# Attention on TensorE: key steps taken in pairs, transposes two steps ahead

## The chip, the cores and the metric

The kernel runs on one core of a Trainium2 chip. The metric is the device time of one execution in microseconds (us). A core has TensorE (PE in the profile; PEld is its loading of weights), VectorE (DVE), ScalarE (ACT), GpSimd (POOL) and SyncE (SP), which issues the DMAs. Each engine works through its own instructions in order and waits on semaphores that other engines raise.

## The reference

A decoder layer: a sparse gated block, cross attention over 1601 keys, and an expert block, each followed by a layer norm. The change lies in the attention, whose core is this, with 32 query heads on 8 key heads of 128, four batches of 256 rows, and keys and queries normalized:

```python
k = _rmsnorm(jnp.repeat(k, GROUPS, axis=1), k_norm_w)
scores = jnp.einsum('bhqd,bhkd->bhqk', q, k) * scale
scores = scores + attention_mask[:, :, :, :kv_len]
probs = jax.nn.softmax(scores.astype(jnp.float32), axis=-1).astype(q.dtype)
out = jnp.einsum('bhqk,bhkd->bhqd', probs, v)
```

## The kernel before, in words

Every product in fp32 precision is made of three products of rounded parts: a number is split into a high part (fp32r) and the low part that is left, and `product` issues high by high, high by low and low by high.

Attention runs over 64 **units**. A unit is half of an item (a batch and a key head): 2 heads x 256 rows, that is four **tiles** j = 0 to 3 of 128 rows by 1601 keys. The hardware loop has trips of four units (`BODY`), u = 0 to 3, and a last trip written out. Within a unit every engine goes through the 13 key steps kt = 0 to 12 (`NT`) of 128 keys, the last of 65, and calls its own `position(i, u, kt)` for each. What an engine does at a position, and in which order, is written by hand:

- PE: `score` at the positions of `AT` (kt 0: tile 1 of the next unit; kt 2: tile 2; kt 5: tile 3; kt 10: tile 0 of the unit after the next): four banks of 402 keys, 12 products, into PSUM banks 0 to 3, which wait for the mask subtraction of the tile before. `weigh_values(kt)`: three products of 512 columns that add values times probabilities to bank 7. `transpose_p`: four transposes of 128 x 128 that turn a step's probabilities of the four tiles into one of three banks (`t_bank`, 4 to 6, in turn). They run `LAG` = 3 steps ahead of the value step, and step 0 of a unit waits (`p_done`) until all four tiles of that unit are normalized. Before it writes a bank, a transpose waits until the low part of the step that used it last is done; in a trip of 52 steps the turn of three doesn't close, so step 0 of a trip waits for the step just before.
- DVE: at kt 0, 3, 5, 8 (`INVERT_AT`) a reciprocal of a tile's sum; at `AT` the mask subtraction with running minimum (`subtract_mask`, L1526), which frees the score's banks; then `split_p`: the low part pT_lo (L1565) of the step that was transposed at this position. For four of the 13 steps (`BY_VECTOR`, the step behind each of `AT`'s positions) DVE also makes the high copy pT_hi (L1561).
- ACT: the high copy pT_hi of the other nine steps (L1495); at kt 12 the copy of bank 7 to o_sb (L1509); at `AT` the exponential of the tile whose mask was subtracted (L1473); at kt 1, 4 and 9 the high part of keys, queries or values of a coming item (`splits`, L1461, L1467).
- POOL: at `INVERT_AT` the product of a tile with its reciprocal (`normalize`, L1419), then low parts of keys, queries or values.
- SP: loads and stores, at kt 1 and kt 12.

The values of a step need its low part (`pT_lo_done`); the splits write into a ring of four (`RING`).

Of the kernel before, what the change touches and what calls it, by code (L numbers as in the profile page):

```python
# [67 lines left out]
def done(step):  # L68

    return AHEAD + 1 + step  # L70
# [42 lines left out]
class Chip:  # L113
# [9 lines left out]
    def sem(self, name):  # L123

        if name not in self.sems:
            self.sems[name] = self.ctx.enter_context(self.nc.semaphore(name))
        return self.sems[name]
# [26 lines left out]
def product(pe, out, a_hi, a_lo, b_hi, b_lo, start, stop):  # L154


    pe.matmul(out, a_hi, b_hi, start=start, stop=False)  # L157
    pe.matmul(out, a_hi, b_lo, start=False, stop=False)  # L158
    return pe.matmul(out, a_lo, b_hi, start=False, stop=stop)  # L159
# [837 lines left out]


def queries(chip, x1T_hi, x1T_lo, WqT, qn, kn, qS, attention):


# [4 lines left out]
    TRIPS = G // 2  # L1006
    LAG = 3
    w_raw = chip.raw[:, 0:2 * CT * W].rearrange("p (r c n) -> p r c n", r=2, c=CT)
# [28 lines left out]
    def last_trip(i):  # L1037
        return isinstance(i, int) and i == TRIPS - 1
# [4 lines left out]
    def upcoming(i, s):  # L1043


        if not last_trip(i) or s + LAG < TT:
            return s + LAG
        return s + LAG - 1 if TT <= s + LAG - 1 < BODY else None

# [57 lines left out]
    def squares(act, i, s):  # L1107
        n = BODY * i + s
        act.wait_ge(q_done, done(n))
        act.wait_ge(ssq_done, done(n - 2))  # L1110
        for h in range(HG):
            last = act.activation(square[:, s % 2, h * HD:(h + 1) * HD], psum[:, bank(i, s), h * HD:(h + 1) * HD],
                                  ACT.Square, accum_out=ssq[:, s % TT, h:h + 1])
        last.then_inc(ssq_done, 1)
# [5 lines left out]
    def scalar(act):  # L1120
# [9 lines left out]

        for s in range(1, LAG):
            squares(act, 0, s)
# [88 lines left out]
def attention(chip, mask, qS, kS, vS, oS, output):  # L1221
# [5 lines left out]
    sem, psum, ident, raw = chip.sem, chip.psum, chip.ident, chip.raw  # L1227
# [4 lines left out]
    SB, SW = 4, 402  # L1232
    KP = SB * SW
    NT = (KV + P - 1) // P
    KR = KV - (NT - 1) * P
    LAG = 3
    TB = 3
    RING = 4
    BODY = 4
    TRIPS = UNITS // BODY  # L1240
    AT = {0: 1, 2: 2, 5: 3, 10: 0}
    INVERT_AT = {0: 0, 3: 1, 5: 2, 8: 3}


    BY_VECTOR = sorted((at + 1 + LAG) % NT for at in AT)
    BY_SCALAR = [kt for kt in range(NT) if kt not in BY_VECTOR]
# [22 lines left out]

    def t_bank(m):  # L1270

        return psum[:, SB + m % (NT * BODY) % TB, :]

    mask_in, k_in, q_in, v_in = (sem(name) for name in ("mask_in", "k_in", "q_in", "v_in"))
    pads, mask_done = sem("pads_a"), sem("mask_done")
# [4 lines left out]
    pT_done, pT_lo_done = sem("pT_done"), sem("pT_lo_done")  # L1280
# [11 lines left out]
    def rows(kt):  # L1292
        return P if kt < NT - 1 else KR

    def schedule(eng, position):

        with eng.Fori(0, TRIPS - 1) as i:
            for u in range(BODY):
                for kt in range(NT):
                    position(i, u, kt)  # L1300
        for u in range(BODY):
            for kt in range(NT):
                position(TRIPS - 1, u, kt)

    def last_trip(i):
        return isinstance(i, int) and i == TRIPS - 1

    def exists(i, u):
        return u < BODY or not last_trip(i)

    def scored(u, kt):

        return (u + 1, AT[kt]) if AT[kt] else (u + 2, 0)

    def transposed(u, kt):

        return (u, kt + LAG) if kt + LAG < NT else (u + 1, kt + LAG - NT)

    def tile(i, u, j):
        return QT * (BODY * i + u) + j  # L1320

    def key_step(i, u, kt):
        return NT * (BODY * i + u) + kt

    def share_step(i, u, kt, share):

        return len(share) * (BODY * i + u) + share.index(kt)
# [194 lines left out]
    def subtract_mask(dve, i, u, j, spare=0):  # L1522
        n = QT * (u % 2) + j

        wait_apart(dve, s_done, done(tile(i, u, j)), dve_passed)
        dve.tensor_tensor_reduce(banked(p_sb[u % 2][:, j]), psum[:, 0:SB, 0:SW],  # L1526
                                 banked(minus_mask[:, j % 2]), 1.0, 3.4028235e38, ALU.add, ALU.min, t_min[:, n:n + 1]
                                 ).then_inc(t_done, 1)

    def invert(dve, i, u, j):  # L1530
        n = QT * (u % 2) + j
        dve.wait_ge(e_done, done(tile(i, u, j)))
        dve.reciprocal(p_inv[:, n:n + 1], p_sum[:, n:n + 1]).then_inc(inv_done, 1)  # L1533
# [21 lines left out]
    def vector(dve):  # L1555
        def split_p(i, u, kt):
            m, n = NT * u + kt, key_step(i, u, kt)
            if kt in BY_VECTOR:
                dve.wait_ge(pT_done, done(n))
                dve.wait_ge(pv_done, done(n - RING))  # L1560
                dve.tensor_copy(pT_hi[0:rows(kt), m % RING], t_bank(m)[0:rows(kt)]).then_inc(pT_hi_dve, 1)  # L1561
                dve.wait_ge(pT_hi_dve, done(share_step(i, u, kt, BY_VECTOR)))
            else:
                dve.wait_ge(pT_hi_act, done(share_step(i, u, kt, BY_SCALAR)))
            dve.tensor_tensor(pT_lo[0:rows(kt), m % RING], t_bank(m)[0:rows(kt)],  # L1565
                              pT_hi[0:rows(kt), m % RING].bitcast(F32), ALU.subtract).then_inc(pT_lo_done, 1)

        def position(i, u, kt):
            if kt in INVERT_AT and exists(i, u + 1):
                invert(dve, i, u + 1, INVERT_AT[kt])  # L1570
            if kt in AT and exists(i, scored(u, kt)[0]):
                subtract_mask(dve, i, *scored(u, kt))
            if exists(i, transposed(u, kt)[0]):
                split_p(i, *transposed(u, kt))
            if last_trip(i) and u >= BODY - 2:
                output.early["vector"](dve, u - BODY, kt)

        for kt in range(LAG):
            split_p(0, 0, kt)
        schedule(dve, position)  # L1580

    def score(pe, i, u, j):
        slot, q = u // 2 % 2, slice(QW * (u % 2) + P * j, QW * (u % 2) + P * (j + 1))
        if j == 0 and u % 2 == 0:
            pe.wait_ge(kq_lo, done(len(KQ) * (2 * i + u // 2 + 1) - 1))
        pe.wait_ge(t_done, done(tile(i, u, j) - 1))
        for b in range(SB):
            k = slice(SW * b, SW * (b + 1))
            last = product(pe, psum[:, b, 0:SW], q_hi[slot][:, q], q_lo[slot][:, q],
                           k_hi[slot][:, k], k_lo[slot][:, k], True, True)  # L1590
        last.then_inc(s_done, 1)
# [9 lines left out]
    def tensor(pe):  # L1601
        def transpose_p(i, u, kt):
            m, n = NT * u + kt, key_step(i, u, kt)
            if kt == 0:
                pe.wait_ge(p_done, done(tile(i, u, QT - 1)))

            pe.wait_ge(pT_lo_done, done(n - 1 if m % (NT * BODY) == 0 else n - TB))
            for j in range(QT):
                last = pe.transpose(t_bank(m)[0:rows(kt), P * j:P * (j + 1)],  # L1609
                                    p_sb[u % 2][:, j, P * kt:P * kt + rows(kt)], ident)  # L1610
            last.then_inc(pT_done, 1)

        def weigh_values(i, u, kt):
            m, n, slot = NT * u + kt, key_step(i, u, kt), u // 2 % 2
            r, d = rows(kt), slice(HD * kt, HD * (kt + 1))
            if kt == 0:
                pe.wait_ge(v_lo_done, done(len(V) * (2 * i + u // 2 + 1) - 1))
                pe.wait_ge(o_done, done(BODY * i + u - 1))
            pe.wait_ge(pT_lo_done, done(n))
            product(pe, o_ps, v_hi[slot][0:r, d], v_lo[slot][0:r, d], pT_hi[0:r, m % RING], pT_lo[0:r, m % RING],  # L1620
                    kt == 0, kt == NT - 1).then_inc(pv_done, 1)

        def position(i, u, kt):
            if kt in AT and exists(i, scored(u, kt)[0]):
                score(pe, i, *scored(u, kt))
            weigh_values(i, u, kt)
            if exists(i, transposed(u, kt)[0]):
                transpose_p(i, *transposed(u, kt))

        pe.wait_ge(sem("qT_sb_done"), done(TT * G - 1))  # L1630
        for kt in range(LAG):
            transpose_p(0, 0, kt)
        schedule(pe, position)

    def open_counts(eng, which):
# [302 lines left out]
def decoder_layer(nc, x, xT, ctxT, mask, WgT, WuT, WdT, WqT, WkT, WvT, WoT, qn, kn, routeT, AT, BwT, out):  # L1938
# [7 lines left out]
    with ExitStack() as whole:  # L1946
# [5 lines left out]

        output = output_and_experts(chip, oS, x1S, WoT, AT, routeT, BwT, out)
        attend = attention(chip, mask, qS.rearrange("b g d h q -> (b g) d (h q)"), kS, vS, oS, output)
        query = queries(chip, x1T_hi, x1T_lo, WqT, qn, kn, qS, attend)
        down = down_and_norm(chip, abs_s, x1T_hi, x1T_lo, x, WdT, pS, x1S, k_sb, query)
# [98 lines left out]
```

## Time and profile before

| | us |
|---|---|
| median of 3 runs | 2784.19 (2783.2 to 2784.31) |
| the profiled execution | 2784.38 |
| its span in the trace | 2782.6 |
| first and last transpose of attention (L1609) | 1059.4 and 2564.6 |
| mean granted clock of TensorE | 0.995 |

The page of a profile gives each engine's busy time as a share of the span; the stretches further down split it by time. A busy PE means that a matmul was in flight. The timeline gives each instruction's start and length. Matmuls overlap, so that the cost of one is the distance from its start to the start of the next.

### The profile page before, as it was taken

What the parts mean: (1) busy time and instruction counts of PE and PEld (TensorE: products, weight loads), DVE (VectorE), ACT (ScalarE), POOL (GpSimd) and SP (SyncE); (2) the same over time, 40 slices, a digit from 0 to 9 for tenths busy, and PEclk for the clock granted to TensorE, in tenths of its full rate; (3) what the DMA queues carried; (4) which work ended last, traced back from release to release, by engine and by line L of the source; (5) the groups of instructions that cost most, each with busy time, mean ns of one, the idle gap of its engine ahead of it and who ended that gap; (6) DMA issues with size and microseconds to landing.
All of it is one profiled execution on the core that took longest, in us unless ns stands there. A gap on an engine that the chain in (4) does not pass through costs nothing.

```text
span 2782.6 us, 45351 instructions
## 1 busy us (share of the span) xinstructions
PE 2738.6 (98%) x14624; PEld 2366.3 (85%) x14624; DVE 2055.9 (74%) x3054; ACT 1362.6 (49%) x2992; POOL 1024.7 (37%) x756
## 2 busy tenths in 40 slices
PE   8999999999999999999999999999999999999998
PEld 7888888888788878889988998988998889888786
DVE  2289999988855566777777777777777777777543
ACT  3243333333424445665666656665666566654421
POOL 1122222222403345454454544454545454541000
PEclk9999999999999999999999999999999999999999
DMA  5253333333333442111111111111111111111632
GB/s 176 81 175 111 104 113 113 106 109 106 97 125 116 125 131 82 63 54 62 54 62 54 62 54 62 54 62 54 61 54 48 57 52 60 54 43 64 205 107 72
DMA packets 252783, 239.49 MB, mean 86 GB/s; under 512 B 12084, under 2 KB 210772, under 8 KB 252728
## 3 DMA queue, kind: packets, MB, share of 16 engines
q1 hardware_dynamic: 252728, 238.81, 27.3%
q8 instruction: 28, 0.46, 0.1%
q14 instruction: 27, 0.22, 0.0%
HBM read 142.92 MB, written 95.85 MB: 86 GB/s over the span
## 4 chain that ended last, share of the span: by engine, by line
PE 96%; issue 2%; POOL 1%; DVE 1%; ACT 0%; DMA 0%; POOLq 0%; SPq 0%; DVEq 0%; ACTq 0%
PE banks L157 27%; PE banks L159 26%; PE banks L158 26%; PE banks L1609 13%; PE banks L323 2%; PE banks L1195 1%; PE banks L930 0%; POOL rstd_q L1095 0%; PE banks L1919 0%; PE banks L1929 0%; DVE p_even L1526 0%; DMA raw<-WoT_in 0%; POOL p_even L1419 0%; POOL x_lo L228 0%; DVE wo_lo L1818 0%
## 5 line engine op out<-in xcount | busy, mean ns | idle before, releaser
L1565 DVE TENSOR_TENSOR pT_lo<-banks,pT_hi 128x512 fp32r<-128x512 f32 (+1 forms) x832 | 573.3, 689 | 111.6 <-ACT pT_hi L1495 94.4
L1495 ACT CAST pT_hi<-banks 128x512 fp32r<-128x512 f32 (+1 forms) x576 | 334.3, 581 | 531.6 <-PE banks L1609 531.5
L560 DVE TENSOR_SCALAR_CACHE_REDUCE flags<-abs_s,cand 128x1376 bf16<-128x1376 f32 x248 | 393.3, 1642 | 1.1
L157 PE MATMUL banks<-pT_hi,v_hi 128*128 128x512 f32 (+1 forms) x832 | 376.1, 452 | 2.9 <-DVE pT_lo L1565 1.6
L157 PE MATMUL banks<-k_hi,q_hi 128*128 128x402 f32 x1024 | 378.8, 370 | 0.0
L158 PE MATMUL banks<-k_lo,q_hi 128*128 128x402 f32 x1024 | 355.4, 347 | 0.0
L159 PE MATMUL banks<-k_hi,q_lo 128*128 128x402 f32 x1024 | 354.3, 346 | 0.0
L159 PE MATMUL banks<-pT_hi,v_lo 128*128 128x512 f32 (+1 forms) x832 | 327.9, 394 | 0.0
L158 PE MATMUL banks<-pT_lo,v_hi 128*128 128x512 f32 (+1 forms) x832 | 326.9, 393 | 0.0
L157 PE MATMUL banks<-kvw_hi,c_hi 128*128 128x512 f32 x816 | 326.1, 400 | 0.0
L158 PE MATMUL banks<-kvw_lo,c_hi 128*128 128x512 f32 x816 | 321.9, 394 | 0.0
L159 PE MATMUL banks<-kvw_hi,c_lo 128*128 128x512 f32 x816 | 321.9, 394 | 0.0
L1419 POOL TENSOR_SCALAR p_even<-p_even,p_inv 128x1601 f32<-128x1601 f32 x128 | 207.2, 1618 | 310.9 <-DVE p_inv L1533 310.9
L1526 DVE CUSTOM_DVE_ANT_0 p_odd<-banks,minus_mask 128x1608 f32<-128x1608 f32 x128 | 234.5, 1832 | 105.5 <-PE banks L159 105.5
L1526 DVE CUSTOM_DVE_ANT_0 p_even<-banks,minus_mask 128x1608 f32<-128x1608 f32 x128 | 234.5, 1832 | 103.5 <-PE banks L159 103.5
L1419 POOL TENSOR_SCALAR p_odd<-p_odd,p_inv 128x1601 f32<-128x1601 f32 x128 | 207.5, 1621 | 211.2 <-DVE p_inv L1533 211.1
L1609 PEld LDWEIGHTS banks<-ident,p_even 128*128 128x128 f32 (+1 forms) x1664 | 207.7, 140 | 58.2 <-DVE qT_sb L1161 2.0
L1609 PEld LDWEIGHTS banks<-ident,p_odd 128*128 128x128 f32 (+1 forms) x1664 | 206.9, 140 | 56.9 <-POOL p_odd L1419 1.0
L1609 PE MATMUL banks<-ident,p_even 128*128 128x128 f32 (+1 forms) x1664 | 249.9, 273 | 1.8 <-DVE qT_sb L1161 1.8
L1609 PE MATMUL banks<-ident,p_odd 128*128 128x128 f32 (+1 forms) x1664 | 249.3, 272 | 0.6 <-POOL p_odd L1419 0.6
L1473 ACT ACTIVATE p_odd<-p_odd,t_min 128x1601 f32<-128x1601 f32 x128 | 209.6, 1637 | 39.9 <-DVE t_min L1526 39.9
L1473 ACT ACTIVATE p_even<-p_even,t_min 128x1601 f32<-128x1601 f32 x128 | 209.6, 1638 | 29.3 <-DVE t_min L1526 29.3
(162 smaller groups left out, 5330.5 us busy)
## 6 DMA issues: line engine op xcount, KB each, us to landing
raw<-keys SPq DMA_DIRECT2D x32, 800.5 KB, 4.5
values<-v_sb SPq DMA_DIRECT2D x50, 512.0 KB, 2.6
keys<-kT_sb SPq DMA_DIRECT2D x50, 512.0 KB, 4.5
raw<-values SPq DMA_DIRECT2D x32, 768.0 KB
queries<-qT_sb SPq DMA_DIRECT2D x64, 256.0 KB, 2.6
raw<-queries SPq DMA_DIRECT2D x32, 512.0 KB, 5.1
attended<-o_sb SPq DMA_DIRECT2D x128, 128.0 KB, 1.8
raw<-attended SPq DMA_DIRECT2D x64, 256.0 KB, 2.9
```

Source lines behind the costliest of these rows:

```text
L157: pe.matmul(out, a_hi, b_hi, start=start, stop=False)
L158: pe.matmul(out, a_hi, b_lo, start=False, stop=False)
L159: return pe.matmul(out, a_lo, b_hi, start=False, stop=stop)
L323: last = pe.transpose(banks[:, g * P:(g + 1) * P], k_sb[:, g * HD:(g + 1) * HD], chip.ident)
L560: bits.done(dve.tensor_scalar(flags[:, tt % 2], abs_s[:, tt], at[:, tt:tt + 1].bitcast(F32), 0.0, ALU.is_lt, ALU.add, accum_out=out[:, tt: ...
L1195: last = pe.transpose(psum[:, bank(i, s), h * P:(h + 1) * P], q_sb[:, s % 4, h * HD:(h + 1) * HD], ident)
L1419: pool.tensor_scalar(at, at, p_inv[:, n:n + 1], 1.0, ALU.mult, ALU.mult).then_inc(p_done, 1)
L1473: act.activation(at, at, ACT.Exp, bias=t_min[:, n:n + 1], scale=-1.0, accum_out=p_sum[:, n:n + 1]).then_inc(e_done, 1)
L1495: act.copy(pT_hi[0:rows(kt), m % RING], t_bank(m)[0:rows(kt)]).then_inc(pT_hi_act, 1)
L1526: dve.tensor_tensor_reduce(banked(p_sb[u % 2][:, j]), psum[:, 0:SB, 0:SW], banked(minus_mask[:, j % 2]), 1.0, 3.4028235e38, ALU.add, ALU.m ...
L1565: dve.tensor_tensor(pT_lo[0:rows(kt), m % RING], t_bank(m)[0:rows(kt)], pT_hi[0:rows(kt), m % RING].bitcast(F32), ALU.subtract).then_inc(p ...
L1609: last = pe.transpose(t_bank(m)[0:rows(kt), P * j:P * (j + 1)], p_sb[u % 2][:, j, P * kt:P * kt + rows(kt)], ident)
```

## The change

The transposes run two steps ahead (`LAG` = 2). PE takes the steps in pairs: at every even step m = 13u + kt it does two transpose groups one after the other, steps m + 2 and m + 3, eight transposes, then the value steps m and m + 1, six products. In units with even u these are the even kt, in the others the odd ones. A score stands ahead of the transposes of its position, except tile 0 (kt 10), which stands behind them. With `LAG` the four steps that DVE copies move from 1, 4, 6, 9 to 0, 3, 5, 8. At odd m, and at kt 10, DVE does the split ahead of the mask subtraction. The last step of a trip uses bank 1 of the three in place of bank 0, and waits for the step two before it.

```diff
--- before.py
+++ after.py
@@ -1233,7 +1233,7 @@
     KP = SB * SW
     NT = (KV + P - 1) // P
     KR = KV - (NT - 1) * P
-    LAG = 3
+    LAG = 2
     TB = 3
     RING = 4
     BODY = 4
@@ -1269,7 +1269,12 @@
 
     def t_bank(m):
 
-        return psum[:, SB + m % (NT * BODY) % TB, :]
+        turn = m % (NT * BODY)
+        return psum[:, SB + (1 if turn == NT * BODY - 1 else turn % TB), :]
+
+    def t_bank_last(m):
+
+        return {NT * BODY - 1: 2, 0: 4, 1: 2, 2: 4}.get(m % (NT * BODY), TB)
 
     mask_in, k_in, q_in, v_in = (sem(name) for name in ("mask_in", "k_in", "q_in", "v_in"))
     pads, mask_done = sem("pads_a"), sem("mask_done")
@@ -1568,9 +1573,12 @@
         def position(i, u, kt):
             if kt in INVERT_AT and exists(i, u + 1):
                 invert(dve, i, u + 1, INVERT_AT[kt])
+            turned_first = (NT * u + kt) % 2 or AT.get(kt) == 0
+            if turned_first and exists(i, transposed(u, kt)[0]):
+                split_p(i, *transposed(u, kt))
             if kt in AT and exists(i, scored(u, kt)[0]):
                 subtract_mask(dve, i, *scored(u, kt))
-            if exists(i, transposed(u, kt)[0]):
+            if not turned_first and exists(i, transposed(u, kt)[0]):
                 split_p(i, *transposed(u, kt))
             if last_trip(i) and u >= BODY - 2:
                 output.early["vector"](dve, u - BODY, kt)
@@ -1604,7 +1612,7 @@
             if kt == 0:
                 pe.wait_ge(p_done, done(tile(i, u, QT - 1)))
 
-            pe.wait_ge(pT_lo_done, done(n - 1 if m % (NT * BODY) == 0 else n - TB))
+            pe.wait_ge(pT_lo_done, done(n - t_bank_last(m)))
             for j in range(QT):
                 last = pe.transpose(t_bank(m)[0:rows(kt), P * j:P * (j + 1)],
                                     p_sb[u % 2][:, j, P * kt:P * kt + rows(kt)], ident)
@@ -1621,11 +1629,21 @@
                     kt == 0, kt == NT - 1).then_inc(pv_done, 1)
 
         def position(i, u, kt):
-            if kt in AT and exists(i, scored(u, kt)[0]):
-                score(pe, i, *scored(u, kt))
+
+            m = NT * u + kt
+            def scores():
+                if kt in AT and exists(i, scored(u, kt)[0]):
+                    score(pe, i, *scored(u, kt))
+
+            if AT.get(kt) != 0:
+                scores()
+            if m % 2 == 0:
+                for ahead in (transposed(u, kt), transposed((m + 1) // NT, (m + 1) % NT)):
+                    if exists(i, ahead[0]):
+                        transpose_p(i, *ahead)
+            if AT.get(kt) == 0:
+                scores()
             weigh_values(i, u, kt)
-            if exists(i, transposed(u, kt)[0]):
-                transpose_p(i, *transposed(u, kt))
 
         pe.wait_ge(sem("qT_sb_done"), done(TT * G - 1))
         for kt in range(LAG):
```

## Rows read from the trace of the kernel before

**Rows 1.** The page, part 1: TensorE's busy time, share of the span, instructions.
```profile
PE 2738.6 (98%) x14624; PEld 2366.3 (85%) x14624; DVE 2055.9 (74%) x3054; ACT 1362.6 (49%) x2992; POOL 1024.7 (37%) x756
```

**Rows 2.** Busy us (x instructions) by engine in the middle of attention, clock, DMA.
```profile
1500.00:2000.00 500.00, 500.00 (x2943) 449.62 (x2942) 394.47 (x614) 302.43 (x434) 244.59 (x139) 1.00 0.18 56
```

**Rows 3.** Timeline, start us and length us: PE's blocks in attention.
```profile
1600.01 0.60 PE L1609 MATMUL banks<-ident,p_even 128*128 128x128 f32 x4
...
1600.36 0.48 PE L157 MATMUL banks<-pT_hi,v_hi 128*128 128x512 f32 x1
...
1600.67 0.39 PE L158 MATMUL banks<-pT_lo,v_hi 128*128 128x512 f32 x1
...
1600.91 0.40 PE L159 MATMUL banks<-pT_hi,v_lo 128*128 128x512 f32 x1
...
1601.14 0.60 PE L1609 MATMUL banks<-ident,p_even 128*65 128x128 f32 x4
...
1601.50 0.43 PE L157 MATMUL banks<-k_hi,q_hi 128*128 128x402 f32 x1
...
1603.78 0.39 PE L157 MATMUL banks<-pT_hi,v_hi 128*128 128x512 f32 x1
```

**Rows 4.** Timeline of PE in the stage of keys: eight transposes in a row.
```profile
500.84 1.03 PE L323 MATMUL banks<-ident,k_sb 128*128 128x128 f32 x8
...
501.63 0.48 PE L157 MATMUL banks<-kvw_hi,c_hi 128*128 128x512 f32 x1
...
501.95 0.39 PE L158 MATMUL banks<-kvw_lo,c_hi 128*128 128x512 f32 x1
```

**Rows 5.** Timeline of an even unit: from score j=3 to the next unit.
```profile
1595.90 0.39 PE L157 MATMUL banks<-pT_hi,v_hi 128*128 128x512 f32 x1
...
1596.26 1.83 DVE L1526 CUSTOM_DVE_ANT_0 p_odd<-banks,minus_mask 128x1608 f32<-128x1608 f32 x1 [0.74 <-PE banks L159]
...
1598.02 0.69 DVE L1565 TENSOR_TENSOR pT_lo<-banks,pT_hi 128x512 fp32r<-128x512 f32 x1
...
1598.13 1.64 ACT L1473 ACTIVATE p_odd<-p_odd,t_min 128x1601 f32<-128x1601 f32 x1 [0.24 <-DVE t_min L1526]
...
1598.62 0.68 DVE L1561 CAST pT_hi<-banks 128x512 fp32r<-128x512 f32 x1
...
1599.33 0.69 DVE L1565 TENSOR_TENSOR pT_lo<-banks,pT_hi 128x512 fp32r<-128x512 f32 x1
...
1599.76 0.57 ACT L1495 CAST pT_hi<-banks 128x512 fp32r<-128x512 f32 x1
...
1600.36 0.69 DVE L1565 TENSOR_TENSOR pT_lo<-banks,pT_hi 128x512 fp32r<-128x512 f32 x1 [0.34 <-ACT pT_hi L1495]
...
1600.97 0.15 DVE L1533 RECIPROCAL p_inv<-p_sum 128x1 f32<-128x1 f32 x1
...
1601.33 1.62 POOL L1419 TENSOR_SCALAR p_odd<-p_odd,p_inv 128x1601 f32<-128x1601 f32 x1 [2.17 <-DVE p_inv L1533]
...
1604.48 0.60 PE L1609 MATMUL banks<-ident,p_odd 128*128 128x128 f32 x4
```

**Rows 6.** Timeline of the odd unit behind it: ACT and DVE round score j=1.
```profile
1607.63 0.57 ACT L1495 CAST pT_hi<-banks 128x512 fp32r<-128x512 f32 x1
...
1608.10 0.59 ACT L1509 COPY o_sb<-banks 128x512 f32<-128x512 f32 x1
...
1608.23 0.69 DVE L1565 TENSOR_TENSOR pT_lo<-banks,pT_hi 128x512 fp32r<-128x512 f32 x1 [0.34 <-ACT pT_hi L1495]
...
1609.74 1.83 DVE L1526 CUSTOM_DVE_ANT_0 p_even<-banks,minus_mask 128x1608 f32<-128x1608 f32 x1 [0.74 <-PE banks L159]
...
1611.61 1.64 ACT L1473 ACTIVATE p_even<-p_even,t_min 128x1601 f32<-128x1601 f32 x1 [0.24 <-DVE t_min L1526]
...
1611.63 0.45 PE L157 MATMUL banks<-k_hi,q_hi 128*128 128x402 f32 x1
...
1613.24 0.85 ACT L1461 CAST k_hi<-raw 128x804 fp32r<-128x804 f32 x1
```

## The prediction

> **What bounds the kernel now.** I read the page first. TensorE is busy for 98% of the span [rows 1]. Then the busy time by stretch: in the middle of attention PE shows 500.00 us of 500, at granted clock 1.00, while DVE shows 394, ACT 302 and POOL 245 [rows 2]. So PE's own work sets attention's time, and a change helps only if it makes that work shorter. It hurts as soon as PE waits, even for an engine that is idle a fifth of the time. That stretch has 2943 products and transposes; a unit (one pass over 13 key steps, with four score tiles) has 48 + 39 + 52 = 139, so a unit takes 500 / (2943/139) = 23.6 us, and the 64 units 1,511 us.
>
> The timeline of PE gives the price of each block from start to start, better than the recorded durations, which overlap. Between the starts of two transpose groups lie 1.13 us (1600.01 to 1601.14) [rows 3]. The three value products start at 1600.36, .67 and .91 and the next group 0.23 later: 0.31, 0.24, 0.23. The first looks 0.08 slow, but its record begins only 0.35 us after the group's start, where four transposes at a pitch of 0.11 would end after 0.44. So the 0.08 belongs to the transposes: a group is 0.436 us, the three products 0.697, together 1.13. A score is twelve products, from 1601.50 to 1603.78, less the same 0.08: 2.20. A unit by these is 4 x 2.20 + 13 x 1.133 = 23.53, so there is less than 0.1 us of waiting in 23.6.
>
> **The change, part by part.** Nothing is computed that wasn't, no DMA moves, and SP's and POOL's queues keep their order. Three things change.
>
> *Pairs of transpose groups.* They halve the passages between transposes and products. What is a passage worth? Another stage of this kernel has eight transposes in a row [rows 4]: 0.79 us to the record of the product behind them, 0.32 to the next. That is 1.11, less a product's 0.23: 0.88 for eight, or 0.110 each. Four in a row cost 0.35 + 0.31 - 0.23 = 0.43, 0.108 each. A passage costs nothing either way, so halving them gains 0. The other bound is to believe the 0.08 us: 416 passages fewer x 0.08 = 33 us gained. I take 0; the row of eight shows the very same 0.08. The Trainium skill (TensorE: Matmul & The Clock Gate, LDWEIGHTS) puts a load of 128 columns at 128/1.2 = 107 ns, whatever else; the pitch of 0.11 agrees, and by it transposes are bound by their loads and the sum's term is also 0.
>
> *LAG 2, the order of the pairs and the four steps that VectorE copies (0, 3, 5, 8 in place of 1, 4, 6, 9).* This changes what lies between a score and the work that hangs on it. The prices of the links are those of the trace, from start to start [rows 5, 6]: score's end to DVE's mask subtraction 0.36 (1595.90 to 1596.26); that to ACT's exponential 1.87, to the next work on DVE about 1.76, to the score that waited for it 1.89 (1609.74 to 1611.63); exponential to the next ACT copy 1.63; copy to the next copy 0.47; copy to DVE's low part 0.60; a DVE copy to its own low part 0.71; a low part to the next DVE instruction 0.61, to PE 0.69 + 0.06 = 0.75 (the 0.06 is what the score needed after the 1.83 of the subtraction); reciprocal to POOL 0.36; POOL's product 1.62.
>
> I call a unit even or odd by u. In an even unit the pairs stand at kt 0, 2, 4 ... 12, in an odd one at 1, 3 ... 11. Going round the two, each wait on PE in turn:
>
> (a) Even unit, kt 5 to 10. From the end of score j=3 the chain is 0.36 + 1.87 + 1.63 + 0.60 (ACT copies step 9 only after the exponential) + 0.61 (DVE reciprocal) + 0.36 + 1.62 + 0.05 = 7.10. In the rows it is 1595.90 to 1601.33 + 1.62 = 1602.95, the same 7.05 [rows 5]. Who waits: the first transposes of the next unit, which need all four normalized tiles. Now they start at 1604.48, 1.5 us after POOL's end, because score j=0 and value step 10 come before them. In the changed kernel they come before both. PE has between: values 5 to 9 and transposes 8 to 12, that is 5 x 0.697 + 5 x 0.436 = 5.67. PE is late by 7.10 - 5.67 = 1.43. In it lie two earlier waits, for the low parts of steps 8 and 9 (3.57 against 3.40 for the second group of the pair at kt 8; 5.21 for value step 9 against 4.70). Behind the waiting transpose stand the score j=0 and everything else on PE, so nothing fills the hole. 1.43 per pair of units.
>
> (b) From that score j=0's end to score j=3 in the odd unit. DVE subtracts at 0.36, the exponential starts at 2.23. Behind it on ACT are, in order, the copy of step 1 (3.86), the copy of o_sb (4.33), the copy of step 2 (4.80). In an odd unit DVE takes step 2 ahead of the subtraction j=1 (the new `turned_first`): low part at 5.40, subtraction at 6.01, where the score's end plus 0.36 would be 5.52. It goes on: exponential 7.88 (score j=2 starts at 7.9), on ACT k_hi (9.51, length 0.85), then the copy of step 4 at 10.3; its low part 10.9 stands again ahead of subtraction j=2: 11.5 instead of 10.5. Score j=3 may start at 11.5 + 1.89 = 13.4. PE's work to there is 8 values, 6 transpose groups, 2 scores: 5.58 + 2.62 + 4.40 = 12.60. Late by 0.8, of which score j=2 waits 0.5 already. Before, the same place cost 0.08. So +0.75.
>
> (c) Odd unit, kt 7. After score j=3 the subtraction starts at 0.7 (DVE still has step 6) and is ahead of step 7's low part, 2.45 to 3.20. The pair at kt 7 needs it for its second group, which PE reaches at 2.7: 0.5. Value step 8 then waits 0.15 more for DVE's copy and low part of step 8. With LAG 3 both had a step more of room. +0.65.
>
> (d) Even unit, kt 4: the second group needs step 4's low part, whose subtraction j=2 came first on DVE: score's end + 0.36 + 1.75 + 0.75 = 2.86, against 2 values, 3 groups = 2.70. +0.16.
>
> *The banks.* The last step of a trip now takes bank 1 and waits for the step two before it in place of three. That step's transposes come in the pair right behind score j=3's chain (c); its low part is about 0.6 us later than PE asks. 16 trips: 16 x 0.6 = 9 us. Nothing covers it, since value step 9, score j=0 and the next unit stand behind it.
>
> Where it costs nothing: value steps 0 to 3, 10, 11 and 12 find their low parts done, since a score (2.20 us) stands between; the first transposes of an even unit come behind a score and value 10, so (a) doesn't appear there; o_sb is copied while score j=1 runs. Their cover is that 2.20 us; without it each would cost up to 0.5 us.
>
> **The sum.** Per two units 1.43 + 0.75 + 0.65 + 0.16 = 2.99 us; 32 of these are 96 us; the banks add 9. The profiled execution took 2784.38 us (span 2782.6) and the median is 2784.19, so nothing is corrected between them: 2784 + 105 = 2889. Bounds: (a) alone is the term whose whole chain stands in the rows, 32 x 1.43 = 46 us, 2830. If each wait also pays for a restart of PE, at most the 0.08 that score j=2 loses now, some 7 waits x 0.08 x 32 = 18 us more: 2908.
>
> **The rivals.**
> R1, only (a) bites. The waits of (b), (c) and (d) come from order on DVE and ACT, and PE is by then later than planned, which gives these engines room that I count only once. For it: DVE is 79% busy, it catches up. Against it: their chains begin at scores, so they shift with PE. 2830 to 2850. Chance 0.18.
> R2, the other side: a passage between transposes and products does cost the 0.08 us and the chains are shorter than I make them. 2784 - 33 = 2751. It decides only if a pair's second group of transposes is followed without loss and (a) is under 1.0 us. Against it: the row of eight [rows 4], and 7.05 us read off directly. 0.05.
> R3, the order does nothing that counts: PE's sequence stays full and passages are free, 2784. It needs slack of 1.4 us at (a) which the rows don't have. 0.05.
> R4, PE's clock falls. The Trainium skill (TensorE: Matmul & The Clock Gate, Part 4) says that transposes don't count as activity for the clock gate. By rows: the clock is 1.00 over 500 us with 37% of the instructions transposes [rows 2], and the change adds none. My waits are below 1.5 us each. Were the clock at half in a tenth of attention, that stretch would cost its own length again, up to 150 us: above 2920. 0.04.
> My forecast, the sum within 2850 to 2920: 0.68.
>
> **The numbers.** 2889 is the likeliest. R1 and the forecast together hold 0.86; from 2828 to 2915 leaves out R2, R3, R4 and the outermost of the forecast, under 2 in 10. Measurement can tell about 0.2%, 5.6 us. Faster 0.05 (R2), same 0.05 (R3), slower 0.90.
>
> **What would show it.** Transpose groups of eight at a pitch of 0.11 and the products behind them with the same 0.48 us record; PE idle at the first transposes of every second unit, released by POOL's normalization, 0.8 us or so there and 1.4 in all since score j=3; waits of scores j=2 and j=3 in odd units for DVE; a period of two units near 50.2 us in place of 47.2; the stages before and after unchanged. I am wrong if PE stays at 100% of attention, if the pitch in groups of eight is below 0.10, or if DVE gets through its queue sooner than the links say.

## The result, and the profile after

The changed kernel takes 2891.22 us (median of 4 runs, 2890.77 to 2892.85), the kernel before 2783.69 on the same chip (4 runs, 2782.29 to 2784.31): a ratio of 1.0388, 95% interval 1.037 to 1.0406. The profiled execution took 2890.95 us.

The page: span, and part 1 (busy time by engine).

```profile
span 2889.2 us, 45396 instructions
...
PE 2795.0 (97%) x14624; PEld 2365.4 (82%) x14624; DVE 2051.9 (71%) x3054; ACT 1339.1 (46%) x2992; POOL 1023.8 (35%) x756
```

The same stretch as in [rows 2], of the changed kernel.

```profile
1500.00:2000.00 500.00, 484.51 (x2741) 418.78 (x2740) 366.36 (x573) 276.31 (x405) 229.50 (x129) 1.00 0.17 53
```

Where 2943 matmuls fitted into 500 us there are 2741, at the same clock: a unit takes 500 / (2741/139) = 25.36 us in place of 23.6, so 1.74 x 64 = 111 us if the whole stage went like this stretch (the stage is measured below). PE isn't full any more (484.51 of 500), and DVE is *less* busy than before. The instructions of the other engines didn't get slower: the mask subtraction takes 1.82 to 1.83 us, the exponential 1.64 and POOL's product 1.61, as before. PE waits.

**Eight transposes in a row** (timeline of PE, changed kernel):

```profile
1600.18 1.03 PE L1617 MATMUL banks<-ident,p_odd 128*128 128x128 f32 x8
1600.97 0.48 PE L157 MATMUL banks<-pT_hi,v_hi 128*128 128x512 f32 x1
1601.29 0.39 PE L158 MATMUL banks<-pT_lo,v_hi 128*128 128x512 f32 x1
```

Start to start 0.79 and 0.32: what the eight of the stage of keys took [rows 4], and per transpose what four took [rows 3]. A pair saves nothing.

**The even unit behind score j=3** (timeline; start, length, and in brackets the idle time and its releaser), against [rows 5]:

```profile
1588.33 1.53 ACT L1500 CAST pT_hi<-banks 128x512 fp32r<-128x512 f32 x3
...
1588.92 0.69 DVE L1570 TENSOR_TENSOR pT_lo<-banks,pT_hi 128x512 fp32r<-128x512 f32 x1 [0.93 <-ACT pT_hi L1500]
...
1589.53 0.15 DVE L1538 RECIPROCAL p_inv<-p_sum 128x1 f32<-128x1 f32 x1
...
1589.67 0.50 PE L157 MATMUL banks<-pT_hi,v_hi 128*128 128x512 f32 x1 [0.27 <-DVE pT_lo L1570]
...
1589.89 1.61 POOL L1424 TENSOR_SCALAR p_odd<-p_odd,p_inv 128x1601 f32<-128x1601 f32 x1 [2.78 <-DVE p_inv L1538]
...
1591.63 0.65 PE L1617 MATMUL banks<-ident,p_odd 128*128 128x128 f32 x4 [0.57 <-POOL p_odd L1424]
```

Three ACT copies sit merged in the first line, since they had waited behind the exponential. Value step 9 starts when step 9's low part (1588.92) is done. The reciprocal, 0.36 behind it POOL, and 1.74 behind POOL's start the transposes of the next unit: 1589.53, 1589.89, 1591.63. Before, those transposes started 1.5 us after POOL's end [rows 5]; now they start 0.13 us after it.

**The odd unit behind it** (timeline of ACT, DVE and PE), against [rows 6]:

```profile
1598.19 0.56 ACT L1500 CAST pT_hi<-banks 128x512 fp32r<-128x512 f32 x1
...
1598.66 0.58 ACT L1514 COPY o_sb<-banks 128x512 f32<-128x512 f32 x1
...
1599.13 0.59 ACT L1500 CAST pT_hi<-banks 128x512 fp32r<-128x512 f32 x1
...
1599.76 0.69 DVE L1570 TENSOR_TENSOR pT_lo<-banks,pT_hi 128x512 fp32r<-128x512 f32 x1 [0.21 <-ACT pT_hi L1500]
...
1600.37 1.82 DVE L1531 CUSTOM_DVE_ANT_0 p_even<-banks,minus_mask 128x1608 f32<-128x1608 f32 x1
...
1602.23 1.64 ACT L1478 ACTIVATE p_even<-p_even,t_min 128x1601 f32<-128x1601 f32 x1 [2.51 <-DVE t_min L1531]
...
1602.26 0.46 PE L157 MATMUL banks<-k_hi,q_hi 128*128 128x402 f32 x1 [0.34 <-DVE t_min L1531]
...
1603.87 0.85 ACT L1466 CAST k_hi<-raw 128x804 fp32r<-128x804 f32 x1
...
1605.23 0.69 DVE L1570 TENSOR_TENSOR pT_lo<-banks,pT_hi 128x512 fp32r<-128x512 f32 x1 [1.70 <-ACT pT_hi L1500]
...
1605.84 1.82 DVE L1531 CUSTOM_DVE_ANT_0 p_even<-banks,minus_mask 128x1608 f32<-128x1608 f32 x1
...
1607.72 0.45 PE L157 MATMUL banks<-k_hi,q_hi 128*128 128x402 f32 x1
```

Behind the exponential come the copy of step 1, the copy of o_sb, the copy of step 2, its low part at 1599.76, and only then the subtraction at 1600.37. The score j=1 ended where value step 0 starts, at 1599.49, and 0.36 behind that would have been 1599.85. Score j=2 starts at 1602.26, 1.89 after the subtraction. Once more: k_hi (1603.87) holds up step 4's copy on ACT, its low part (1605.23) stands ahead of the subtraction (1605.84), and score j=3 waits until 1607.72.

**The other places** (timeline of PE: kt 7 and 8 of that odd unit, where the second transpose group starts 0.79 behind the first in place of 0.44; then kt 9 of the last unit of a trip, where it is 0.91, the wait for a bank):

```profile
1612.30 0.60 PE L1617 MATMUL banks<-ident,p_odd 128*128 128x128 f32 x4
1613.09 0.66 PE L1617 MATMUL banks<-ident,p_odd 128*128 128x128 f32 x4 [0.19 <-DVE pT_lo L1570]
1613.50 0.47 PE L157 MATMUL banks<-pT_hi,v_hi 128*128 128x512 f32 x1
...
1614.41 0.50 PE L157 MATMUL banks<-pT_hi,v_hi 128*128 128x512 f32 x1
```

```profile
1665.65 0.60 PE L1617 MATMUL banks<-ident,p_odd 128*128 128x128 f32 x4
1666.56 0.65 PE L1617 MATMUL banks<-ident,p_odd 128*65 128x128 f32 x4 [0.30 <-DVE pT_lo L1570]
```

Who waited for whom in attention (us in total, times, longest):

```profile
PE banks L1617 <- POOL p_odd L1424: 17.6, 32, 0.6
PE banks L1617 <- DVE pT_lo L1570: 15.1, 48, 2.7
PE banks L157 <- DVE t_min L1531: 10.4, 31, 0.3
PE banks L157 <- DVE pT_lo L1570: 9.1, 33, 0.4
```

These rows add up to 52 us, half of what was lost. The record of a value product lasts 0.39 us where the next starts 0.23 behind it, so the recorded ends reach some 0.16 us beyond the slot, and a wait is partly or wholly covered by its forerunner's record. The loss has to be read from starts. I did that for all 1,915 blocks of PE in attention, with the prices of the prediction (group 0.436, three products 0.697, score 2.20; behind transposes the start is taken from the second product): each block's start less the former's start and price. A block right behind a waiting one starts 0.06 us late by this measure as well; that is the 0.06 in the rows.

| place | predicted, us | measured mean, us |
|---|---|---|
| (a) even: second group at kt 8, value 8, value 9, first transposes of the next unit | 1.43 | 0.18 + 0.06 + 0.54 + 0.71 = 1.49 |
| (b) odd: scores j=2, j=3, less 0.09 before | 0.75 | 0.61 + 0.29 - 0.09 = 0.81 |
| (c) odd: second group at kt 7, values 7 and 8 | 0.65 | 0.34 + 0.06 + 0.23 = 0.63 |
| (d) even: second group at kt 4, value 4 | 0.16 | 0.16 + 0.06 = 0.22 |
| banks, once a trip | 0.6 | 0.46 |
| all of attention | 105 | 122.7 - 13.9 = 108.8 |

The 13.9 are the same sum in the kernel before; 5.5 of it is score j=2's wait, most of the rest lies in the first and the last unit. From the start of attention's first block to that of its last it is 1508.0 us before and 1616.9 after, the same difference. The places (a) to (d) and the banks make 32 x 3.15 + 16 x 0.46 = 108 us of it. The rest of the span is 2.3 us shorter than before, so that the profiled executions differ by 106.6. The banks' 0.46 is the typical value, found in 15 of the 16 trips; in the last one, which is written out, it is 1.98 us, and the shortened exponential further down leaves it there.

### The profile page after: what moved, and what is told of

Read it like the earlier page. It is cut to its first block, busy times and chain, and to the rows that moved or that the text cites. A ratio compares the mean times of both kernels' runs of the same rounds, so it can differ in the third digit from the quotient of the medians.

```text
span 2889.2 us, 45396 instructions
## 1 busy us (share of the span) xinstructions
PE 2795.0 (97%) x14624; PEld 2365.4 (82%) x14624; DVE 2051.9 (71%) x3054; ACT 1339.1 (46%) x2992; POOL 1023.8 (35%) x756
## 4 chain that ended last, share of the span: by engine, by line
PE 82%; issue 8%; ACT 3%; DVE 3%; POOL 3%; DMA 0%; ACTq 0%; DVEq 0%; POOLq 0%; SPq 0%
PE banks L157 23%; PE banks L159 23%; PE banks L158 23%; PE banks L1617 10%; ACT pT_hi L1500 2%; POOL p_odd L1424 2%; PE banks L323 2%; DVE p_even L1531 1%; DVE pT_lo L1570 1%; PE banks L1195 1%; ACT o_sb L1514 1%; DVE p_inv L1538 0%; PE banks L930 0%; ACT p_even L1478 0%; POOL rstd_q L1095 0%
## 5 line engine op out<-in xcount | busy, mean ns | idle before, releaser
L1500 ACT CAST pT_hi<-banks 128x512 fp32r<-128x512 f32 (+1 forms) x576 | 323.7, 580 | 123.7 <-PE banks L1617 121.1
L157 PE MATMUL banks<-k_hi,q_hi 128*128 128x402 f32 x1024 | 368.0, 359 | 11.4 <-DVE t_min L1531 10.4
L157 PE MATMUL banks<-pT_hi,v_hi 128*128 128x512 f32 (+1 forms) x832 | 367.1, 441 | 9.8 <-DVE pT_lo L1570 9.1
L1617 PE MATMUL banks<-ident,p_odd 128*128 128x128 f32 (+1 forms) x1664 | 229.9, 275 | 29.6 <-POOL p_odd L1424 17.6
L1617 PEld LDWEIGHTS banks<-ident,p_odd 128*128 128x128 f32 (+1 forms) x1664 | 191.6, 140 | 71.5 <-DVE pT_lo L1570 46.9
L1617 PE MATMUL banks<-ident,p_even 128*128 128x128 f32 (+1 forms) x1664 | 232.3, 275 | 5.5 <-DVE pT_lo L1570 3.1
L157 PEld LDWEIGHTS banks<-k_hi,q_hi 128*128 128x128 f32 x1024 | 193.2, 189 | 51.5 <-DVE t_min L1531 46.0
```

Source lines behind the costliest of these rows:

```text
L1500: act.copy(pT_hi[0:rows(kt), m % RING], t_bank(m)[0:rows(kt)]).then_inc(pT_hi_act, 1)
```

## The experiments

Theory A is the prediction's: PE's blocks need low parts, free banks and normalized tiles whose chains begin at a score; the new order asks for them sooner, and PE waits for the difference. Theory B is that one of the two halves of the change alone is the cause, first the pairs, then the shorter lead. Ratios are to the kernel before, run on the same chip.

**Lead alone.** LAG 2 in the kernel before, no pairs; tile 0's score and subtraction behind the transposes of kt 10.

```diff
-    LAG = 3
+    LAG = 2
...
-            if kt in AT and exists(i, scored(u, kt)[0]):
+            if AT.get(kt) and exists(i, scored(u, kt)[0]):
                 score(pe, i, *scored(u, kt))
             weigh_values(i, u, kt)
             if exists(i, transposed(u, kt)[0]):
                 transpose_p(i, *transposed(u, kt))
+            if AT.get(kt) == 0 and exists(i, scored(u, kt)[0]):
+                score(pe, i, *scored(u, kt))
...
+            turned_first = AT.get(kt) == 0
+            if turned_first and exists(i, transposed(u, kt)[0]):
+                split_p(i, *transposed(u, kt))
             if kt in AT and exists(i, scored(u, kt)[0]):
                 subtract_mask(dve, i, *scored(u, kt))
-            if exists(i, transposed(u, kt)[0]):
+            if not turned_first and exists(i, transposed(u, kt)[0]):
```

> The kernel before with LAG 2 and no pairs; only tile 0's score and its mask subtraction go behind the transposes of kt 10, which need their data. Theory A (the loss comes from work that hangs on a score and now has a step less of room): behind score j=3 value step 7 waits 0.6 us and step 8 0.2, behind j=2 step 4 waits 0.6, score j=2 itself 0.3; 1.6 us a unit more than before, 64 units, so about 2885 us, as much as the changed kernel, though there are no pairs. PE waits for low parts, none for POOL's normalization. Theory B (it is the pairs themselves: eight transposes and then six products hold PE's partners up): 2784 to 2800 us.

Measured: 2956.82 us, ratio 1.0621 (1.0605 to 1.0637). That the pairs alone are the cause falls: without a pair the loss is not smaller but 66 us larger. Yet my size missed by 72 us. The waits of this kernel in attention, and one of them in PE's timeline:

```profile
PE banks L157 <- DVE pT_lo L1565: 67.4, 180, 1.6
...
PE banks L157 <- ACT o_sb L1509: 20.5, 60, 1.2
```

```profile
1607.85 0.60 PE L1612 MATMUL banks<-ident,p_even 128*128 128x128 f32 x4
1608.88 0.50 PE L157 MATMUL banks<-pT_hi,v_hi 128*128 128x512 f32 x1 [0.43 <-DVE pT_lo L1565]
```

By block starts each unit loses 2.8 us, where I had 1.7 with what it lost before: value steps 4 and 7 wait 0.69 each (I said 0.6), step 8 0.19; score j=2, from which I expected 0.3, doesn't wait; but step 9 waits 0.41 and step 10 0.12, which I had missed, and value step 0 waits 0.60 for ACT's copy of o_sb, which stands behind the exponential. In the changed kernel value step 10 stands behind tile 0's score, here ahead of it, so that 0.7 us less work lies between that score and value step 0; and a pair's two groups lie between a score and the values that follow in half of the cases. So the short lead costs by itself. That the changed kernel loses less with the same lead fits these differences of order, but no run separates them.

**Pairs with the old lead.** The changed kernel with LAG 3, tile 0's score ahead of the transposes again, and with it its mask subtraction in even units. With LAG the four steps that DVE copies move back to 1, 4, 6, 9.

```diff
-    LAG = 2
+    LAG = 3
...
-            turned_first = (NT * u + kt) % 2 or AT.get(kt) == 0
+            turned_first = (NT * u + kt) % 2
...
-            if AT.get(kt) != 0:
-                scores()
+            scores()
             if m % 2 == 0:
...
-            if AT.get(kt) == 0:
-                scores()
```

> The changed kernel with LAG 3: pairs of steps m + 3 and m + 4. Theory A: the lead of three doesn't save it, since the second of a pair comes up to a step earlier than before. The first transposes of a unit now stand in odd units at kt 9, 4.97 us behind score j=3, with the chain to POOL's end at 7.1: a wait of 2.1 us there; scores j=2 and j=3 of odd units 1.1 in all, 0.6 more in small waits: some 3.8 us per two units, about 2900 us (2870 to 2920). Theory B (the loss is the shorter lead alone, pairs are harmless): 2784 to 2800 us. A theory that passages cost 0.08 us each would give 2751 where no wait is added.

Measured: 2888.89 us, ratio 1.038 (1.0365 to 1.0396), 11 us less than I expected. Its largest wait in attention:

```profile
PE banks L1617 <- POOL p_even L1424: 48.8, 31, 1.8
```

The first transposes, now at kt 9 of odd units, lose 1.76 us by block starts (I said 2.1), score j=3 of odd units 0.30 and score j=2 nothing new (I said 1.1 for both), small waits and the banks the rest. Lead 3 doesn't save pairs: the first transposes of a unit are pulled ahead of tile 0's score in one unit of two, by either way. So that the shorter lead alone is the cause falls too. Each half of the change by itself costs as much as the whole or more (lead 174 us, pairs 106, both 107): they don't add. That fits Theory A, as both take away blocks of PE between a score and the work that hangs on it.

**The chain to POOL, made shorter.** Changed kernel, tile 3's reciprocal and normalization at kt 7.

```diff
-    INVERT_AT = {0: 0, 3: 1, 5: 2, 8: 3}
+    INVERT_AT = {0: 0, 3: 1, 5: 2, 7: 3}
```

> The changed kernel, with the reciprocal and normalization of tile 3 at kt 7 in place of kt 8, ahead of step 9's split on DVE. Theory A: the chain behind score j=3 gets about 1 us shorter (7.1 to 6.1), the wait for POOL at the first transposes of an odd unit goes, the one of value step 9 (0.5) stays: 0.75 us less in each of 32 even units, 24 us, so about 2867 us. If POOL's end isn't what PE waits for there, 2891 us.

Measured: 2865.56 us, ratio 1.03 (1.0286 to 1.0314): 25.7 us less than the changed kernel. Timeline round the first transposes, and what PE still waits for in attention:

```profile
1580.73 0.17 DVE L1538 RECIPROCAL p_inv<-p_sum 128x1 f32<-128x1 f32 x1 [0.47 <-ACT p_odd L1478]
...
1581.10 1.62 POOL L1424 TENSOR_SCALAR p_odd<-p_odd,p_inv 128x1601 f32<-128x1601 f32 x1 [1.73 <-DVE p_inv L1538]
...
1583.18 0.60 PE L1617 MATMUL banks<-ident,p_odd 128*128 128x128 f32 x4
```

```profile
PE banks L1617 <- DVE pT_lo L1570: 13.6, 49, 1.8
...
PE banks L157 <- DVE t_min L1531: 10.2, 31, 0.4
PE banks L157 <- DVE pT_lo L1570: 9.2, 33, 0.4
```

POOL starts at 1581.10 and ends at 1582.72; the transposes follow at 1583.18 without a wait, and the row for POOL is gone. By block starts 0.71 falls to nothing, value step 9 keeps its 0.54.

**The same wait, covered instead.** Changed kernel, tile 0's score between the two groups of kt 10 in even units.

```diff
-                for ahead in (transposed(u, kt), transposed((m + 1) // NT, (m + 1) % NT)):
+                for at, ahead in enumerate((transposed(u, kt), transposed((m + 1) // NT, (m + 1) % NT))):
+                    if AT.get(kt) == 0 and at == 1:
+                        scores()
                     if exists(i, ahead[0]):
                         transpose_p(i, *ahead)
-            if AT.get(kt) == 0:
+            elif AT.get(kt) == 0:
                 scores()
```

> The changed kernel, with the score of tile 0 between the two transpose groups of kt 10 in even units, so that 2.2 us of products stand ahead of the first transposes of the next unit. Theory A: the wait for POOL there (0.7) goes, value step 9's 0.5 stays: 0.75 us less; and the score's subtraction and exponential start 0.44 us earlier against the rest, which shortens score j=2's wait in the odd unit by about as much: together 1.2 us per two units, 38 us, about 2853 us (2850 to 2870). If the wait for POOL isn't the cause of the hole there, 2891 us.

Measured: 2855.85 us, ratio 1.0259 (1.0245 to 1.0273), 35 us less than the changed kernel. The wait at the first transposes is gone, and score j=2's fell from 0.61 to 0.16, by 0.45, as worked out: the chain (b) starts a transpose group earlier against PE.

**Both cures.** The two edits above together.

> The changed kernel with both cures of the first transposes of an odd unit: reciprocal and normalization of tile 3 at kt 7, and the score of tile 0 ahead of these transposes. Theory A: the two take away the same wait for POOL, so they don't add; what is left (value step 9's 0.5, step 8's low part) neither touches: 2855 us, as with the score alone. If they were two causes, 2856 - 25 = 2831 us.

Measured: 2854.13 us, ratio 1.025 (1.0233 to 1.0267). They don't add: it was one wait, between a chain that ends at POOL and the blocks that PE has until then. One cure shortens the chain, the other puts more blocks ahead of its end.

**DVE's order.** Changed kernel, mask subtraction ahead of the split except at kt 10.

```diff
-            turned_first = (NT * u + kt) % 2 or AT.get(kt) == 0
+            turned_first = AT.get(kt) == 0
```

> The changed kernel with the mask subtraction ahead of the split at kt 0, 2 and 5 of every unit, as before the change (kt 10 stays turned). Theory A: in odd units score j=2 no longer waits (0.5 less), but value step 4 then waits 0.6 for its low part, so little is gained there; at kt 7 of odd units 0.3 less. In even units the wait only moves from value step 9 to the second group of kt 8. About 0.45 us less per two units, 14 us: 2877 us (2865 to 2890). Rival, that the turned order is what costs most: below 2850 us.

Measured: 2881.17 us, ratio 1.035 (1.0336 to 1.0365), 10 us less than the changed kernel, where I expected 14. The waits in attention:

```profile
PE banks L157 <- DVE pT_lo L1570: 26.9, 64, 0.4
PE banks L1617 <- POOL p_odd L1424: 15.9, 32, 0.5
...
PE banks L1617 <- DVE pT_lo L1570: 9.0, 19, 1.8
```

No row for t_min is left: the scores wait no more than in the kernel before. In exchange values wait for low parts three times as long (26.9 us here, 9.1 in the changed kernel): by block starts value step 4 of odd units 0.67. One wait moved: in even units 0.69 turned up at value step 7, not at kt 8 as I had said, with which the wait of value step 9 went. So most of it only moved; net the turned order costs 10 us.

**The exponential, cut short.** Both kernels, exponential over 800 of 1601 columns; the rest of the softmax's numerator and sum is left out.

```diff
-        at = p_sb[u % 2][:, j, 0:KV]
+        at = p_sb[u % 2][:, j, 0:KV // 2]
         act.wait_ge(t_done, done(tile(i, u, j)))
```

> The changed kernel; the exponential covers only the first 800 of 1601 columns, so about 0.82 us less on ACT each time; the other columns keep the masked scores (that part of the softmax is left out). PE's work is the same. Theory A (PE waits for chains that run through the exponential): POOL's end behind score j=3 comes at 6.3 in place of 7.1, value step 9's wait goes: 0.8 us less in each even unit; scores j=2 and j=3 of odd units, whose chain holds two exponentials, no longer wait: 0.8 less; the wait of step 8's low part in odd units and the banks' wait nearly go: 0.6 less. About 2.3 us per two units, 74 us, and 9 at the banks: 2808 us (2800 to 2825). Rival (the losses come from DVE's order and the turned blocks of PE alone): above 2870.

> The control: the same shortened exponential in the kernel before. PE is full there and the one wait, score j=2's, is for a mask subtraction that no exponential precedes: 2784 us, within 3.

Measured: 2832.8 us, ratio 1.0174 (1.0157 to 1.0191), and for the kernel before 2784.08 us, ratio 1.0001 (0.9991 to 1.001). In the timeline the exponential takes 0.96 where it took 1.64:

```profile
1607.11 0.96 ACT L1478 ACTIVATE p_odd<-p_odd,t_min 128x800 f32<-128x800 f32 x1 [0.93 <-DVE t_min L1531]
```

The waits of PE for POOL and for low parts at transposes:

```profile
PE banks L1617 <- POOL p_odd L1424: 13.8, 32, 0.6
...
PE banks L1617 <- DVE pT_lo L1570: 4.2, 4, 1.8
```

58 us came back in the changed kernel and none in the kernel before, so more than half of the loss is PE waiting for chains that run through ACT's exponential. I had expected 83. Three terms were too large: the exponential got 0.68 us shorter, not 0.82, so (a) fell from 1.49 to 0.18 + 0.06 + 0.59 = 0.83, by just those 0.66, all of value step 9's wait and little of the first transposes'; and value step 8 of odd units keeps its 0.23, since its chain (subtraction, low part of step 7, copy and low part of step 8, all on DVE) has no exponential in it; and the second group at kt 7 keeps 0.14 of its 0.34. With the banks, where no more than 7.4 of 9 us could come back, and a slip in my own sum (0.8, 0.8 and 0.6 make 2.2, not 2.3) this is some 22 of the 25 us. Scores j=2 and j=3 of odd units lost their waits as expected (0.90 to 0.08).

**Passages, twice as many.** The kernel before, each four transposes split in two and two by the third value product.

```diff
+            pe.matmul(o_ps, v_hi[slot][0:r, d], hi, start=kt == 0, stop=False)
+            pe.matmul(o_ps, v_hi[slot][0:r, d], lo, start=False, stop=False)
...
+            transpose_half(v, w, range(2))
+            pe.matmul(o_ps, v_lo[slot][0:r, d], hi, start=False, stop=kt == NT - 1).then_inc(pv_done, 1)
+            transpose_half(v, w, range(2, QT)).then_inc(pT_done, 1)
```

> The kernel before, with each group of four transposes split in two: after the second of a value step's three products come two transposes, then the third product, then the other two. Same work and waits, twice the passages between transposes and products (832 more). Theory A (a passage costs nothing): 2784 us, within 4. Rival (the 0.08 us by which the record of the first product behind transposes is longer is real): 832 x 0.08 = 67 us more, 2851 us.

Measured: 2785.51 us (11 runs), ratio 1.0004 (0.9995 to 1.0013). One value step of its timeline:

```profile
1600.17 0.38 PE L1614 MATMUL banks<-ident,p_even 128*128 128x128 f32 x2
1600.30 0.48 PE L1634 MATMUL banks<-pT_hi,v_lo 128*128 128x512 f32 x1
...
1600.76 0.48 PE L1627 MATMUL banks<-pT_hi,v_hi 128*128 128x512 f32 x1
...
1601.30 0.38 PE L1614 MATMUL banks<-ident,p_even 128*65 128x128 f32 x2
```

Both products behind transposes now show the long record (0.48), and a step still takes 1.13 us (1600.17 to 1601.30). So the long record means that it begins early, 0.13 us behind two transposes that take 0.22; the passage is free.

**The one wait of the kernel before.** Its score of kt 2 behind value step 2.

```diff
+            if kt == 2:
+                weigh_values(i, u, kt)
             if kt in AT and exists(i, scored(u, kt)[0]):
                 score(pe, i, *scored(u, kt))
-            weigh_values(i, u, kt)
+            if kt != 2:
+                weigh_values(i, u, kt)
```

> The kernel before, with the score of kt 2 behind value step 2 in place of ahead of it. Theory A: that score is the one place where PE waits in the kernel before, 0.08 us for the subtraction of the tile ahead, 64 times; 0.7 us of products now stand ahead of it. 5 us less, 2779 us, if the score's later end puts off nothing (tile 2's exponential starts 0.7 us later; step 4's low part, which stands behind the subtraction on DVE, has three steps of room). Rival: the waits return at value step 5 or score j=3, 2784 us or more.

Measured: 2779.13 us (11 runs, 2776.85 to 2780.02), ratio 0.998 (0.9971 to 0.9989). Value step 2, then the score, at PE's plain pitch:

```profile
1609.93 0.48 PE L157 MATMUL banks<-pT_hi,v_hi 128*128 128x512 f32 x1
1610.25 0.39 PE L158 MATMUL banks<-pT_lo,v_hi 128*128 128x512 f32 x1
1610.48 0.40 PE L159 MATMUL banks<-pT_hi,v_lo 128*128 128x512 f32 x1
1610.71 0.34 PE L157 MATMUL banks<-k_hi,q_hi 128*128 128x402 f32 x1
```

It beats both kernels, by the 5 us that the wait was worth.

## Why the prediction was right, point by point

- *Passages cost nothing.* Right, twice: eight in a row keep the pitch of 0.11, and 832 passages more cost nothing.
- *(a)* Right in place and size, 1.49 for 1.43. That its last part, 0.71 at the first transposes, is the chain to POOL, is shown by shortening it (25.7 us) and by covering it; the two don't add. The extra 0.06 is value step 8's late start behind a waiting block, which I had put only into the upper bound. The split was less exact than the sum: value step 9 waits 0.54 where I had 0.34 (5.21 - 4.70 less the 0.17 of kt 8), so 0.2 less was left for the first transposes (0.71 for 0.92).
- *(b)* Right in size, 0.81 for 0.75 (13.4 - 12.60 - 0.08, as it stands in the prediction, is 0.72). Score j=2 waits at 1.89 behind the late subtraction, as worked out. That its chain runs through ACT, the short exponential shows.
- *(c), (d)* Right in size, 0.63 and 0.22 for 0.65 and 0.16. Of (c) the short exponential takes 0.20 away and leaves value step 8's 0.23, which fits a chain on DVE alone. (d) was read from starts and not tried by an edit of its own.
- *Banks.* 0.46 for 0.6, 7.4 us in place of 9; read from the trace. No edit went to the turn of the banks itself; with the short exponential the wait is gone, so it too hangs on a chain through ACT.
- *R1*, only (a) bites: fell: (b) to (d) make 1.66 of the 3.15 us per two units. Their chains begin at scores and so move with PE. *R2* and *R3* fell with the passages and with (a). *R4*: the clock stayed at 1.00 through the whole stretch.
- *The sum.* 105 predicted, 107.5 measured. Small misses of both signs cancel in it ((a), (b) and (d) up, (c) and the banks down, the rest of the kernel 2.3 us shorter), so it looks a little better than its terms are; that is luck. The same working missed by 72 us when I used it for the lead alone, where I had gone through scores and low parts but not through the copy of o_sb and the later value steps.

What stays open: how the 66 us between the lead alone and the changed kernel divide. The two differ in the pairs, in the place of value step 10, in DVE's turned order at odd steps and in the banks at the end of a trip. Of these only DVE's order was tried by itself, in the changed kernel, where it costs 10 us.

## What to carry to other kernels

When an engine is full, a new order of its work can gain no more than the waits that it has (here 5 us), as long as passages between kinds of work are free. Before changing the order, write down for each block what it waits for and how long that chain is from the last block of the full engine that feeds it; then count the blocks in between in the new order. Shorter queues of ready work (a lead of two for three, or a pair that asks for its second member early) are paid for at every place where the chain is longer than the blocks. Measure a full engine from start to start: here a passage that looks 0.08 us dear in the records was free.

## What the runs showed that I had not expected

The idle time of PE in the records is half of what it loses: 52 us in the rows against 109 by starts, since matmul records overlap by about 0.16 us. And the shorter lead costs more in an order without pairs (174 us) than in the one with them (107 us), while pairs lose about the same with a lead of three (106 us) as with two.
